# Two heads' scores in 64-row tiles, queries scaled on the way out of PSUM, and probabilities rescaled on POOL alone

## What is computed

```python
def _L1_xattn_ref(x, context, Wq, Wk, Wv, Wo, bo):
    HEADS, DIM_HEAD = 8, 64
    scale = DIM_HEAD ** (-0.5)
    q = (x @ Wq).reshape(b, n, HEADS, DIM_HEAD).transpose(0, 2, 1, 3)
    k = (context @ Wk).reshape(b, m, HEADS, DIM_HEAD).transpose(0, 2, 1, 3)
    v = (context @ Wv).reshape(b, m, HEADS, DIM_HEAD).transpose(0, 2, 1, 3)
    scores = jnp.einsum('bhnd,bhmd->bhnm', q, k) * scale
    attn = jax.nn.softmax(scores, axis=-1)
    out = jnp.einsum('bhnm,bhmd->bhnd', attn, v)
    return out.transpose(0, 2, 1, 3).reshape(b, n, HIDDEN) @ Wo + bo
...
x = x + jnp.tanh(g_xattn[0]) * _L0_xattn_ref(_layernorm(x), ctx, ctx, ...)
x = x + jnp.tanh(g_ffn[0]) * _L0_ffn_ref(_layernorm(x), ...)
x = x + jnp.tanh(g_xattn[1]) * _L1_xattn_ref(_layernorm(x), ctx, ...)
x = x + jnp.tanh(g_ffn[1]) * _L1_ffn_ref(_layernorm(x), ...)   # router, 2 of 8 experts a batch
```

## Time and profile before

| what | value |
|---|---|
| three timed runs | 284.59, 287.31, 287.57 us; the median is 287.31 |
| span of the profiled execution | 285.0 us, first to last instruction |
| that span against the median of the runs | 0.992 |
| PE, DVE, ACT, POOL busy | 234.1, 200.8, 136.7, 94.2 us |
| PE's granted clock, mean | 0.941 of full speed |

### The profile page before, as it was taken

How to read it: one execution, slowest core, us unless ns; L and a number is a source line. 1 busy time by engine, 2 the same in 40 slices (tenths; PEclk the granted TensorE clock), 3 DMA queues, 4 the chain that set the end, 5 groups by cost and what they waited for, 6 DMA issues and landing times.

```text
span 285.0 us, 4711 instructions
## 1 busy us (share of the span) xinstructions
PE 234.1 (82%) x1686; PEld 178.3 (63%) x1686; DVE 200.8 (70%) x498; ACT 136.7 (48%) x345; POOL 94.2 (33%) x129
## 2 busy tenths in 40 slices
PE   0912889489889999879789699989979968999992
PEld 0712655366666575668668477867757746799891
DVE  4699975458886435998847988796997983245643
ACT  2610434146455664435539657676655621726440
POOL 4699300033434353033445623231241150021111
PEclk9965999979999999999999989999999975999998
DMA  7830999600000000000000000000400401300510
GB/s 193 226 31 22 204 217 222 115 0 5 3 3 2 5 0 2 0 1 2 0 0 0 3 0 2 1 0 0 149 0 3 147 1 18 133 0 2 166 30 25
DMA packets 11986, 13.79 MB, mean 48 GB/s; under 512 B 1028, under 2 KB 9988, under 8 KB 11676
## 3 DMA queue, kind: packets, MB, share of 16 engines
q1 hardware_dynamic: 11676, 12.96, 18.7%
q10 hardware_dynamic: 288, 0.54, 0.9%
HBM read 9.70 MB, written 2.88 MB: 44 GB/s over the span
## 4 chain that ended last, share of the span: by engine, by line
PE 56%; DVE 28%; DMA 7%; ACT 3%; issue 2%; SPq 2%; POOL 1%; POOLq 0%; DVEq 0%; ACTq 0%
PE PS L1194 7%; PE PS L1241 6%; PE PS L1255 5%; DVE XH L714 5%; PE PS L1226 4%; PE PS L1134 4%; DVE QK L820 4%; PE PS L1210 3%; DMA QK<-MT 2%; DVE MX L808 2%; DMA X<-in_x 2%; PE PS L1056 2%; PE PS L1060 2%; PE PS L1109 2%; DVE MX L751 2%
## 5 line engine op out<-in xcount | busy, mean ns | idle before, releaser
L751 DVE TENSOR_REDUCE MX<-PS 128x2 f32<-128x512 f32 (+1 forms) x48 | 31.7, 686 | 13.1 <-PE PS L1091 7.7
L1194 PE MATMUL PS<-KT,VA 128*128 128x256 f32 x128 | 32.3, 396 | 1.4 <-ACT VA L652 1.3
L456 POOL TENSOR_TENSOR QK<-QK,RC 128x512 f32<-128x512 f32 x16 | 16.7, 1042 | 44.7 <-DVE RC L816 44.7
L595 ACT ACTIVATE QK<-PS,NM 128x256 f32<-128x256 f32 x64 | 29.4, 477 | 1.1 <-DVE NM L810 1.1
L1194 PEld LDWEIGHTS PS<-KT,VA 128*128 128x128 f32 x128 | 23.7, 195 | 8.6 <-issue 4.1
L446 POOL TENSOR_SCALAR_AFFINE_SELECT PT<-PT 128x512 f32<-128x512 f32 x16 | 10.1, 634 | 54.3 <-ACT PT L575 54.3
L571 ACT ACTIVATE PT<-PS 128x1024 f32<-128x1024 f32 x16 | 16.4, 1023 | 24.1 <-PE PS L1109 24.1
L808 DVE TENSOR_REDUCE MX<-PS 128x4 f32<-128x1024 f32 x16 | 19.5, 1218 | 11.7 <-PE PS L1194 11.6
L409 POOL TENSOR_SCALAR VE<-MV 128x2 f32<-128x2 f32 x20 | 5.2, 259 | 64.7 <-DVE MV L704 64.7
L820 DVE TENSOR_SCALAR QK<-QK,RC 128x256 f32<-128x256 f32 x32 | 25.4, 832 | 0.6
L714 DVE TENSOR_SCALAR XH<-X,MV,RS 128x128 f32<-128x128 f32 x32 | 20.2, 1018 | 2.3 <-POOL RS L410 2.3
(11 more groups left out here) (175 smaller groups left out, 544.4 us busy)
## 6 DMA issues: line engine op xcount, KB each, us to landing
QK<-in_w SPq DMA_DIRECT2D x8, 512.0 KB, 4.2
QK<-qk_scr SPq DMA_DIRECT2D x3, 768.0 KB, 9.0
qk_scr<-V SPq DMA_DIRECT2D x2, 768.0 KB, 7.7
W<-in_w SPq DMA_DIRECT2D x1, 768.0 KB, 7.4
QK<-PARTS SPq DMA_DIRECT2D x12, 64.0 KB
qk_scr<-PARTS SPq DMA_DIRECT2D x1, 768.0 KB, 5.4
X<-in_x SPq DMA_DIRECT2D x2, 256.0 KB, 5.5
CT<-in_ctxT SPq DMA_DIRECT2D x2, 256.0 KB, 6.8
```

The source lines that it names most:

```text
L456: g_.tensor_tensor(pr, pr, RC1[:, n % 2, 2:4].unsqueeze(2).to_broadcast([P, 2, S]), ALU.mult).then_inc(s_p1p, 1)
L595: last = a.activation(PR[:, n % 3, h, it, :], banks(2 * (n % 2) + h)[:, it * S:(it + 1) * S], ACT.Exp, scale=D1 ** -0.5, bias=NM1[:, n % 2 ...
L751: v.tensor_reduce(dst, banks(n % 2).rearrange("p (h j) -> p h j", j=w), AXX, ALU.max, negate=True).then_inc(s_mx0, 1)
L1194: last = mm(banks(2 * (n % 2) + h)[:, it * S:(it + 1) * S], QT1[:, c, h, it * P:(it + 1) * P], KT1[:, c, b * S:(b + 1) * S], start=True, s ...
```

## The change

There are five edits, all in the second layer's attention.

1. The scores use 64-row tiles. Each product reads its head's own 64 rows of queries and keys, at rows 0 or 64, and the loop has the query halves outside and the heads inside. There are still four products, each of 128 by 256 outputs, and the two heads write different PSUM banks. `QT1` becomes half as large and has no zeros.
2. The memset of `QT1` on POOL goes, with its semaphore `s_qz`.
3. The event `q` copies all 128 rows of PSUM in one ACT instruction in place of two of 64 rows, and scales by `D1 ** -0.5` in it.
4. The maxima are taken of scaled scores, so the scaling L810 goes and the exponentials carry no scale.
5. `normalise1` on DVE keeps the reciprocals alone. POOL divides the probabilities of both heads, one after the other, and T waits for two counts of `s_p1p`.

```diff
-        QT1 = VAF[:, 0:2048].rearrange("p (c h s) -> p c h s", c=4, h=2)
+        QT1 = VAF[:, 0:1024].rearrange("p (c s) -> p c s", c=4)
...
                 pool.wait_ge(s_rc1, n + 1)
-                pr = PR[:, n % 3, 1]
-                g_.tensor_tensor(pr, pr, RC1[:, n % 2, 2:4].unsqueeze(2).to_broadcast([P, 2, S]),
-                                 ALU.mult).then_inc(s_p1p, 1)
+                for h in range(2):
+                    pr = PR[:, n % 3, h]
+                    g_.tensor_tensor(pr, pr, RC1[:, n % 2, 2 * h:2 * h + 2].unsqueeze(2).to_broadcast([P, 2, S]),
+                                     ALU.mult).then_inc(s_p1p, 1)
...
-                if g == E0 + 5:
-
-                    pool.wait_ge(s_av0, 4 * B)
-                    g_.memset(VAF[:, 0:2048], 0.0).then_inc(s_qz, 1)
...
-                                            scale=D1 ** -0.5, bias=NM1[:, n % 2, 2 * h + it:2 * h + it + 1],
+                                            bias=NM1[:, n % 2, 2 * h + it:2 * h + it + 1],
...
-                        act.wait_ge(s_qz, 1)
+                        act.wait_ge(s_av0, 4 * B)
                     wait_misc("q", b, j)
-                    for h in range(2):
-                        rows = slice(64 * h, 64 * h + 64)
-                        last = a.activation(QT1[rows, 2 * j:2 * j + 2, h, :],
-                                            misc[rows].rearrange("p (c t) -> p c t", c=2), ACT.Copy)
-                    last.then_inc(s_q1, 1)
+                    a.activation(QT1[:, 2 * j:2 * j + 2, :], misc.rearrange("p (c t) -> p c t", c=2), ACT.Copy,
+                                 scale=D1 ** -0.5).then_inc(s_q1, 1)
...
-                link(v.tensor_reduce(MX1[:, k, :], banks(2 * k, 1024).rearrange("p (c j) -> p c j", j=S),
-                                     AXX, ALU.max, negate=True))
-                v.tensor_scalar(NM1[:, k, :], MX1[:, k, :], D1 ** -0.5, None, ALU.mult).then_inc(s_nm1, 1)
+                v.tensor_reduce(NM1[:, k, :], banks(2 * k, 1024).rearrange("p (c j) -> p c j", j=S),
+                                AXX, ALU.max, negate=True).then_inc(s_nm1, 1)
...
                 v.reciprocal(RC1[:, k, :], SM1[:, k, :]).then_inc(s_rc1, 1)
-                dve.wait_ge(s_rc1, n + 1)
-                for it in range(2):
-                    pr = PR[:, n % 3, 0, it, :]
-                    last = v.tensor_scalar(pr, pr, RC1[:, k, it:it + 1], None, ALU.mult)
-                last.then_inc(s_p1, 1)
...
-                for h in range(2):
-                    for it in range(2):
+                for it in range(2):
+                    for h in range(2):
+                        rows = slice(64 * h, 64 * h + 64)
                         last = mm(banks(2 * (n % 2) + h)[:, it * S:(it + 1) * S],
-                                  QT1[:, c, h, it * P:(it + 1) * P], KT1[:, c, b * S:(b + 1) * S],
+                                  QT1[rows, c, it * P:(it + 1) * P], KT1[rows, c, b * S:(b + 1) * S],
                                   start=True, stop=True)
...
             def transpose_p(n):
-                pe.wait_ge(s_p1, n + 1)
-                pe.wait_ge(s_p1p, n + 1)
+                pe.wait_ge(s_p1p, 2 * n + 2)
```

More of the change, by code:

```diff
@@ L222, in build_program @@
         HT = BIGF[:, 14336:16384].rearrange("p (a f s) -> p a f s", a=2, f=FT)
-        MX1 = sb("MX1", [P, 2, 4])
         NM1 = sb("NM1", [P, 2, 4])
@@ L262, in build_program @@
         d_w1, d_ab, d_late = map(sem, ("d_w1", "d_ab", "d_late"))
-        s_cst, s_tanh, s_qz = map(sem, ("s_cst", "s_tanh", "s_qz"))
+        s_cst, s_tanh = map(sem, ("s_cst", "s_tanh"))
         s_xbo = sem("s_xbo")
@@ L291, in build_program @@
         s_ce, s_cg, s_ln, s_ws = map(sem, ("s_ce", "s_cg", "s_ln", "s_ws"))
-        s_s1, s_nm1, s_e1, s_p1, s_t1, s_pt1a, s_pt1d, s_av1, s_ot1 = map(
-            sem, ("s_s1", "s_nm1", "s_e1", "s_p1", "s_t1", "s_pt1a", "s_pt1d", "s_av1", "s_ot1"))
+        s_s1, s_nm1, s_e1, s_t1, s_pt1a, s_pt1d, s_av1, s_ot1 = map(
+            sem, ("s_s1", "s_nm1", "s_e1", "s_t1", "s_pt1a", "s_pt1d", "s_av1", "s_ot1"))
         s_q1, s_lgr, s_er, s_idx, s_dd, s_e2, s_oh, s_oht, s_b1s = map(
```

## The result

The changed kernel took 272.12 us on the median of four runs (268.18 to 280.49), the kernel before 287.44 beside it: ratio 0.9377, 95% interval [0.926, 0.9495]. A later job timed it again: 272.78 us on the median of six (270.15 to 276.6), ratio 0.9539 [0.9468, 0.9609]. The ratios leave out the executions that were slower at a lower granted clock, the medians do not, so a ratio is not quite the quotient of its medians. It is faster, by more than I forecast: 276.5 would be a ratio of 0.962, outside both intervals. In the profiled execution (270.65 us) the span went from 285.0 to 268.9, 16.1 less where my sum said 10.5.

What follows compares the result with a forecast made beforehand. PE was taken to bound 162 to 200 us, DVE and its loop 200 to 231. Gains 2.4 + 4.4 + 5.2 = 12.0, less 1.5, gave 10.5 us off the 287.31 median: forecast 276.5, range 270 to 284.

Steps and rivals of the forecast that it cites:

- my sum: Whole kernel: stretch gains of 12.0 us, less 1.5 for DVE waiting for POOL, gave 10.5 us.
- The third change of layout: On PE, the step after the scores now enters from another layout, costing 0.15 us.
- The sum's 0.72 a unit: Scores with the step after them on PE: 64-row tiles gain 0.72 us for each of 16 units.
- the 1.5 that I took off: Second layer's attention: DVE's SBUF-only instructions wait while POOL divides, costing 1.5 us in all.
- the term up to T(2): Head of the stage, to near 168 us: earlier `q` copies and cheaper scores gain 2.4 us.
- The three terms up to T(14): Gains of 2.4 us to T(2), 4.4 to 200 us, and 5.2 from there to T(14) at 230.45.
- Rival (a): From S(5) on, the loop through POOL sets the pace; 281 us, chance 0.16.
- rival (b): In the scores, 64-row tiles don't run side by side; 285 us on the median, chance 0.10.
- The step that failed: From T(14) at 230.45 us on, order, waits and half clock stay the same; gain 0.
- rival (d): Before T(14), the wait shrinks with DVE light, and the half clock behind it; 272 us, chance 0.08.
- Rival (c): Across PE's steps, more and longer waits drop its clock to half; 290 us or above, chance 0.06.

Runs made afterwards that it cites:

- run 6: Changed kernel with the score products of both heads in rows 0 to 63; 282.9 to 296.6 us, median 287.0, ratio not given.
- 10: Kernel before, unchanged, profiled a second time; ratio 1.0044 to the other runs of that kernel.
- 9: Changed kernel, unchanged, profiled a second time and timed again; median 272.78 us of six, ratio 0.9539.
- 2: Kernel before with the division of both heads on POOL as the only change; ratio 0.9706.
- 3: Changed kernel with the old division put back, one head on DVE and one on POOL; ratio 0.9695.
- 4: Kernel before with unused products filling PE's two long waits, at the stage's head and before T(14); ratio 0.9888.
- 11: Changed kernel with unused products filling PE's waits at 157 us (six) and 217 us (four); 272.45 us, ratio 0.9578.
- 5: Changed kernel with the heads as the outer loop of the score products; ratio 0.9546.

## Why the prediction was right, and where it was wrong

The direction was right, and so was what I said of the single edits; the time was forecast too high by a term that I had put at nothing.

**Edit 1** was right in its mechanism. S is 1.06, where I had 1.05, with the two halves of the array side by side (run 6). The third change of layout costs less than I put down: nothing for T, 0.20 for `q` (1.06 for 0.86) and 0.20 for `wo1` (1.98). The sum's 0.72 a unit was so 0.86 where T follows and 0.66 where `q` or `wo1` does. The drain at a change of mode that the Trainium skill, page "TensorEngine Tiling (Array Packing)", section "Key Properties", names, without a time, shows in two of the three kinds of neighbour (if these 0.20 us are that drain) and not in the third.

**Edit 5** was right too. The division pair takes 2.05, DVE's busy time fell by 25.4 us (200.85 to 175.5; I had said 26), and the loop held the pace of PE from 166 to 194. The L707 pair at the head, beside POOL's division, took 2.05 in place of 0.59: this is the 1.5 that I took off for DVE waiting for POOL, nearly all in one place (a second pair took 1.24 and is not in the chain, the others 0.59 to 0.60). But there the edit also gives something that I had not booked. In the kernel before the pair stood behind L820 and L826 and started at 160.59; now nothing of the division is ahead of it on DVE and it starts at 157.84, 2.75 sooner. So the 1.5 was paid and more than given back: the pair ends at 159.89 where it ended at 161.18. Taking it off the sum was wrong, since the term up to T(2) came out at 2.50 with it paid.

**The three terms up to T(14)**, 2.4, 4.4 and 5.2, were measured as 2.50, 4.07 and 5.69. That they agree so closely is in part luck: in the second pair of executions (10 and 9) the sum is 7.9 in place of 12.3, for half clock alone. Rival (a), a loop through POOL that sets the pace, and rival (b), tiles one after the other, are refuted by these and by run 6.

**The step that failed** is "From 230.45 on the order and the waits are the same: 0", with its reason that the half clock "stays, since it follows a wait of PE of the same 2.60 us". The order is the same, the wait was not: 1.75 us. I had priced the latency of the division there, rightly as unchanged, and took the wait to be that latency. A wait is the latency less what PE has still to do when it starts, and that had grown from 1.02 to 1.76 us. The half clock did not stay either: 6.63 us from T(14) to T(15) for 10.90. That was rival (d), to which I gave 0.08, with 272 us.

How much of the 16.1 that is can be told only roughly. The profiled pair shows 4.27 us, the second pair 2.81 (9.44 less 6.63). The table gives 8.81 less 6.88, 1.9 us, from waits of 2.6 to waits of 1.4 to 1.8, each over executions that scatter by 1 to 4 us and over different kernels. The rest, 2.3, is that my one profile of before had the longest half clock of five at that place; I had read it as the price of the place. As an estimate for the medians, 12.3 and 1.9 are 14.2, and the medians differ by 15.3 and 14.2 us (287.44 less 272.12; 286.95 less 272.78). This is near, but the 1.9 rests on five and seven executions, and the 12.3 is 7.9 in the second pair. That the failed step is the shorter wait is shown by runs 2 and 3; how many us of half clock it saves on the average stays open.

**Rival (c)**, slower by the clock, did not come, but a small form of it did. In the second execution of after half clock fell at two more places of the stage without a new wait, 3.0 us to T(14) against the first (76.55 less 73.59); what brings it at one of these places and not in the other execution is not settled. Nor is what brings it behind T(14) once the wait there is filled (4, 11): the short waits of 0.26 and 0.66 and the small products of 8 rows there (L1298) are what is left. They stand ahead of the second half clock in all seven executions that have it, and in those that don't have it too, and no run took them away.

## What to carry to other kernels

Price a wait as the latency less the work that the waiting engine still has, and work that out again after the change, above all where half clock may follow. Before a stretch at half clock is booked as a fixed cost, profile the kernel a second time; it is a draw. A short filler in the one wait of over 2.5 us, and products that wait for another engine moved behind work that doesn't, took 3.2 us off the way to T(14); neither by itself, nor for certain both together, could be told from after in the timed runs.

## What the runs showed of the hardware

- Two fp32 products of 64 rows in different halves of TensorE take the time of one: eight of 256 columns in 1.06 us (after), 1.92 if all are in one half (6). This holds too if the program gives all of one half first (5: 1.07). The Trainium skill, page "TensorE: Matmul & The Clock Gate", section "The mechanism", has products start strictly in program order; by that rule the first product of the second half would start three products of 0.216 us later than in pairs, 1.7 us for S, an estimate; the trace shows 1.07 and disagrees.
- Granted clock: behind waits of PE of 2.87 to 3.71 us it fell to the lower level at once in nine places of nine, behind 2.03 to 2.64 in five of nine, behind 1.39 to 1.78 in none of seven at T(14) and in two of eight at L1290 (1.55), and in none of the five places where the wait was filled. It also fell some 5 to 7 us behind T(14), ahead of which stood eight small products and waits of 0.26 to 0.66 us, in seven executions of fifteen.
- DVE's pair L707 took 2.05 us beside 2.04 us of POOL's division, and 0.59 to 0.60 in five places of seven. DVE's copy out of PSUM (L813) took 674 ns on the mean with two divisions of POOL a step, and 679 (L826) with one.
